# Twelve weight loads per chunk, each cut in two halves issued one step apart

## The reference

```
x = x + 0.5 * ffn(layernorm(x))
x = x + mamba(layernorm(x))
x = x + 0.5 * ffn(layernorm(x))

ffn:    xr, xk = mixes of x and of x one token earlier
        out = sigmoid(xr @ W_r.T) * ((relu(xk @ W_k.T) ** 2) @ W_v.T)
mamba:  xn = layernorm(x) * ln_w + ln_b ;  xs, z = split(xn @ W_in.T)
        xc = silu(causal conv of 4 taps over xs)
        dt_low, B, C = split(xc @ W_xproj.T) ;  delta = softplus(dt_low @ W_dt.T + b_dt)
        h[t] = exp(delta * A) * h[t-1] + delta * B * xc        (1024 channels, 16 states)
        y = sum over states(h * C) + D_skip * xc ;  out = (y * silu(z)) @ W_out.T + x
```

## Time and profile before

| what | value |
|---|---|
| runs | 4676.57, 4679.0, 4679.5 us (median 4679.0) |
| the profiled execution, its own time | 4679.25 us |
| its span, first to last instruction | 4677.5 us |
| mean granted TensorE clock | 0.974 |
| busy: PE / DVE / POOL / ACT | 4190.6 / 4202.4 / 3559.8 / 3164.0 us |
| DMA of the kernel's queue | 807.00 MB, 54.1% of the 16 engines' span |

### The profile page before, as it was taken

How to read it: one execution, slowest core, us unless ns; L and a number is a source line. 1 busy time by engine, 2 the same in 40 slices (tenths; PEclk the granted TensorE clock), 3 DMA queues, 4 the chain that set the end, 5 groups by cost and what they waited for, 6 DMA issues and landing times.

```text
span 4677.5 us, 58356 instructions
## 1 busy us (share of the span) xinstructions
PE 4190.6 (90%) x16768; PEld 2358.7 (50%) x16768; DVE 4202.4 (90%) x3266; ACT 3164.0 (68%) x6740; POOL 3559.8 (76%) x3712
## 2 busy tenths in 40 slices
PE   5777999999999999999999999999999999999787
PEld 2444555555555555555455555555555555555453
DVE  1799999999999999999999999999999999999991
ACT  3666677767767677667767767776776767766562
POOL 2677787877878778787788878787787887878771
PEclk8888999999999999999999999999999999999798
DMA  2455555555655555565555655556565555655551
GB/s 76 125 158 185 177 180 181 178 195 167 192 180 178 173 181 195 181 194 177 182 173 181 198 177 180 181 178 195 168 192 181 178 176 182 193 179 167 159 184 55
DMA packets 423058, 810.74 MB, mean 173 GB/s; under 512 B 41265, under 2 KB 41265, under 8 KB 418641
## 3 DMA queue, kind: packets, MB, share of 16 engines
q1 hardware_dynamic: 422736, 807.00, 54.1%
HBM read 772.25 MB, written 34.60 MB: 172 GB/s over the span
## 4 chain that ended last, share of the span: by engine, by line
PE 45%; DVE 24%; issue 12%; POOL 8%; ACT 7%; DMA 3%; SPq 0%; DVEq 0%; POOLq 0%; ACTq 0%
DVE decay L1099 13%; PE mm L478 9%; PE y_acc L573 9%; PE mm L489 8%; DVE g L1107 7%; POOL dbx L1306 6%; PE mm L515 5%; PE mm L500 4%; PE mm L602 3%; DVE xc L1051 3%; DMA c_all<-bc_scratch 3%; PE mm L525 3%; PE mm L537 2%; POOL xin L1295 1%; PE mm L464 1%
## 5 line engine op out<-in xcount | busy, mean ns | idle before, releaser
L1306 POOL TENSOR_TENSOR dbx<-u,b_all 128x1024 f32<-128x1024 f32 x1024 | 2417.9, 2361 | 187.0 <-DVE g L1107 183.6
L1099 DVE TENSOR_TENSOR_SCAN decay<-decay,state,dbx 128x1024 f32<-128x1024 f32 x1024 | 2406.9, 2350 | 155.2 <-ACT decay L913 131.7
L1107 DVE TENSOR_TENSOR g<-decay,c_all 128x1024 f32<-128x1024 f32 x1024 | 1246.3, 1217 | 57.7 <-PE y_acc L573 45.0
L573 PE MATMUL y_acc<-ident,g 128*128 128x128 f32 x8192 | 1077.8, 279 | 238.2 <-DVE g L1107 235.8
L573 PEld LDWEIGHTS y_acc<-ident,g 128*128 128x128 f32 x8192 | 950.3, 143 | 657.9 <-DVE g L1107 384.8
L910 ACT ACTIVATE decay<-delta,neg_a 128x512 f32<-128x512 f32 x1024 | 708.5, 692 | 37.1 <-ACT state L919 0.4
L919 ACT ACTIVATE state<-decay 128x2 f32<-128x2 f32 x1024 | 167.9, 164 | 782.5 <-DVE g L1107 780.0
L913 ACT ACTIVATE decay<-delta,neg_a 128x511 f32<-128x511 f32 x1024 | 687.1, 671 | 0.0
L500 PE MATMUL mm<-wbuf_c,col 128*128 128x512 f32 x1024 | 458.2, 593 | 9.6 <-ACT delta L861 8.2
L1051 DVE SCALAR_TENSOR_TENSOR xc<-mm,conv_sb,xc 128x509 f32<-128x509 f32 (+2 forms) x384 | 285.3, 743 | 50.4 <-ACT xs_last L825 41.4
L500 PEld LDWEIGHTS mm<-wbuf_c,col 128*128 128x128 f32 x1024 | 187.4, 190 | 214.7 <-issue 212.5
(11 more groups left out here) (107 smaller groups left out, 5377.0 us busy)
## 6 DMA issues: line engine op xcount, KB each, us to landing
b_all<-bc_scratch SPq DMA_DIRECT2D x1024, 256.0 KB, 3.7
c_all<-bc_scratch SPq DMA_DIRECT2D x1024, 256.0 KB, 4.0
wbuf_d<-in_w_r SPq DMA_DIRECT2D x32, 1024.0 KB, 7.1
wbuf_c<-in_w_v SPq DMA_DIRECT2D x32, 1024.0 KB, 7.7
xin<-in_x SPq DMA_DIRECT2D x16, 1024.0 KB, 7.0
wbuf_c<-in_w_k SPq DMA_DIRECT2D x16, 1024.0 KB, 5.6
wbuf_d<-in_w_in SPq DMA_DIRECT2D x16, 1024.0 KB, 8.2
res_scratch<-rows SPq DMA_DIRECT2D x16, 1024.0 KB, 6.2
```

What stands on the lines that cost most here:

```text
L573: last = pe.matmul(y_acc[:, tb, j * P:(j + 1) * P], g[:, s % PAIRS, j, tb * P:(tb + 1) * P], ident[:, :], start=n == 0 and j == 0 and tb % ...
L1099: dve.tensor_tensor_scan(d, d, flat(dbx[:, s % DBX, :, :]), state[:, batch, s, 0:1], ALU.mult, ALU.add).then_inc(scan_done, 1)
L1107: dve.tensor_tensor(g[:, s % PAIRS, :, :], decay[:, s % PAIRS, :, :], c_all[:, s % CRING, :].unsqueeze(1).broadcast_to([P, QT, W]), ALU.mu ...
L1306: pool.tensor_tensor(dbx[:, s % DBX, :, :], u[:, q % 2, :, :], b_all[:, s % BRING, :].unsqueeze(1).broadcast_to([P, QT, W]), ALU.mult).the ...
```

## The change

The piece of 512 x 512 becomes two of 256 rows: a helper `half` takes the place of `piece`. The first half stands where the load stood, behind the same wait. The second half is issued one step later, without a wait of its own, behind that step's `c_all` and `b_all`. Both halves add 16 to the same semaphore, and each reader waits for twice the count. This is done for all twelve loads. Three of them, and one of the readers, are shown; the others follow the same pattern.

```diff
-            def piece(dram, rows0, cols0):
-                return dram[rows0:rows0 + 512, cols0:cols0 + 512].rearrange("(t p) n -> p t n", p=P)
+            def half(dram, rows0, cols0):
+                return dram[rows0:rows0 + 256, cols0:cols0 + 512].rearrange("(t p) n -> p t n", p=P)
...
                     if back and s == LOAD["wo1"]:
                         after(mark(z_pe, b, "7"))
-                        sp.dma_start(wbuf["b"][:, :, :], piece(w_out, 512, 0)).then_inc(wo_loaded[1], 16)
+                        sp.dma_start(wbuf["b"][:, 0:2, :], half(w_out, 512, 0)).then_inc(wo_loaded[1], 16)
+                    if back and s == min(LOAD["wo1"] + 1, NSTEP - 1):
+                        sp.dma_start(wbuf["b"][:, 2:4, :], half(w_out, 768, 0)).then_inc(wo_loaded[1], 16)
                     if back and s == LOAD["res"]:
...
                     if scn and s == LOAD["wz0"]:
                         after(mark(f_pe[0], f, "v3") if front else mark(f_pe[1], it - 2, "v3"))
-                        sp.dma_start(wbuf["c"][:, :, :], piece(w_in, 0, E)).then_inc(wz_loaded[0], 16)
+                        sp.dma_start(wbuf["c"][:, 0:2, :], half(w_in, 0, E)).then_inc(wz_loaded[0], 16)
+                    if scn and s == min(LOAD["wz0"] + 1, NSTEP - 1):
+                        sp.dma_start(wbuf["c"][:, 2:4, :], half(w_in, 256, E)).then_inc(wz_loaded[0], 16)
...
                             after((f_pe[1].sem, count))
-                        sp.dma_start(wbuf["d"][:, :, :], piece(w_r, 0, 0)).then_inc(wr_loaded[1], 16)
+                        sp.dma_start(wbuf["d"][:, 0:2, :], half(w_r, 0, 0)).then_inc(wr_loaded[1], 16)
+                    if back and s == min(LOAD["wr1"] + 1, NSTEP - 1):
+                        sp.dma_start(wbuf["d"][:, 2:4, :], half(w_r, 256, 0)).then_inc(wr_loaded[1], 16)
...
-                pe.wait_ge(wo_loaded[part], 16 * (k + 1))
+                pe.wait_ge(wo_loaded[part], 32 * (k + 1))
```

More of the change, by code:

```diff
@@ L380, in body @@
                         after(mark(f_pe[0], f, "k3"))
-                        sp.dma_start(wbuf["c"][:, :, :], piece(w_v, 0, 0)).then_inc(wv_loaded[0], 16)
+                        sp.dma_start(wbuf["c"][:, 0:2, :], half(w_v, 0, 0)).then_inc(wv_loaded[0], 16)
+                    if front and s == min(LOAD["wv0"] + 1, NSTEP - 1):
+                        sp.dma_start(wbuf["c"][:, 2:4, :], half(w_v, 256, 0)).then_inc(wv_loaded[0], 16)
                     if front and s == LOAD["wxs0"]:
                         after(mark(f_pe[0], f, "r3"))
-                        sp.dma_start(wbuf["d"][:, :, :], piece(w_in, 0, 0)).then_inc(wxs_loaded[0], 16)
+                        sp.dma_start(wbuf["d"][:, 0:2, :], half(w_in, 0, 0)).then_inc(wxs_loaded[0], 16)
+                    if front and s == min(LOAD["wxs0"] + 1, NSTEP - 1):
+                        sp.dma_start(wbuf["d"][:, 2:4, :], half(w_in, 256, 0)).then_inc(wxs_loaded[0], 16)
                     if scn and s == LOAD["wz0"]:
                         after(mark(f_pe[0], f, "v3") if front else mark(f_pe[1], it - 2, "v3"))
-                        sp.dma_start(wbuf["c"][:, :, :], piece(w_in, 0, E)).then_inc(wz_loaded[0], 16)
+                        sp.dma_start(wbuf["c"][:, 0:2, :], half(w_in, 0, E)).then_inc(wz_loaded[0], 16)
+                    if scn and s == min(LOAD["wz0"] + 1, NSTEP - 1):
+                        sp.dma_start(wbuf["c"][:, 2:4, :], half(w_in, 256, E)).then_inc(wz_loaded[0], 16)
                     if back and s == LOAD["wk1"]:
                         after(mark(y_pe, b, "o3"))
-                        sp.dma_start(wbuf["b"][:, :, :], piece(w_k, 0, 0)).then_inc(wk_loaded[1], 16)
+                        sp.dma_start(wbuf["b"][:, 0:2, :], half(w_k, 0, 0)).then_inc(wk_loaded[1], 16)
+                    if back and s == min(LOAD["wk1"] + 1, NSTEP - 1):
+                        sp.dma_start(wbuf["b"][:, 2:4, :], half(w_k, 256, 0)).then_inc(wk_loaded[1], 16)
                     if front and s == LOAD["wxs1"]:
@@ L395, in body @@
                             after(mark(m_pe, f - 1, "xs7"))
-                        sp.dma_start(wbuf["a"][:, :, :], piece(w_in, 0, 512)).then_inc(wxs_loaded[1], 16)
+                        sp.dma_start(wbuf["a"][:, 0:2, :], half(w_in, 0, 512)).then_inc(wxs_loaded[1], 16)
+                    if front and s == min(LOAD["wxs1"] + 1, NSTEP - 1):
+                        sp.dma_start(wbuf["a"][:, 2:4, :], half(w_in, 256, 512)).then_inc(wxs_loaded[1], 16)
                     if front and s == LOAD["res_out"]:
@@ L402, in body @@
                         after(mark(z_pe, it, "3") if scn else mark(f_pe[1], b - 1, "v3"))
-                        sp.dma_start(wbuf["c"][:, :, :], piece(w_v, 0, 0)).then_inc(wv_loaded[1], 16)
+                        sp.dma_start(wbuf["c"][:, 0:2, :], half(w_v, 0, 0)).then_inc(wv_loaded[1], 16)
+                    if back and s == min(LOAD["wv1"] + 1, NSTEP - 1):
+                        sp.dma_start(wbuf["c"][:, 2:4, :], half(w_v, 256, 0)).then_inc(wv_loaded[1], 16)
                     if back and s == LOAD["wr1"]:
@@ L414, in body @@
                             after(mark(y_pe, b, "o3"))
-                        sp.dma_start(wbuf["a"][:, :, :], piece(w_out, 0, 0)).then_inc(wo_loaded[0], 16)
+                        sp.dma_start(wbuf["a"][:, 0:2, :], half(w_out, 0, 0)).then_inc(wo_loaded[0], 16)
+                    if scn and s == min(LOAD["wo0"] + 1, NSTEP - 1):
+                        sp.dma_start(wbuf["a"][:, 2:4, :], half(w_out, 256, 0)).then_inc(wo_loaded[0], 16)
                     if scn and s == LOAD["wz1"]:
@@ L418, in body @@
                             after(mark(f_pe[1], b, "k3"))
-                        sp.dma_start(wbuf["b"][:, :, :], piece(w_in, 0, E + 512)).then_inc(wz_loaded[1], 16)
+                        sp.dma_start(wbuf["b"][:, 0:2, :], half(w_in, 0, E + 512)).then_inc(wz_loaded[1], 16)
+                    if scn and s == min(LOAD["wz1"] + 1, NSTEP - 1):
+                        sp.dma_start(wbuf["b"][:, 2:4, :], half(w_in, 256, E + 512)).then_inc(wz_loaded[1], 16)
                     if front and s == LOAD["bc_out"]:
@@ L434, in body @@
                             after(mark(m_pe, f, "xs3"))
-                        sp.dma_start(wbuf["d"][:, :, :], piece(w_r, 0, 0)).then_inc(wr_loaded[0], 16)
+                        sp.dma_start(wbuf["d"][:, 0:2, :], half(w_r, 0, 0)).then_inc(wr_loaded[0], 16)
+                    if ahead and s == min(LOAD["wr0"] + 1, NSTEP - 1):
+                        sp.dma_start(wbuf["d"][:, 2:4, :], half(w_r, 256, 0)).then_inc(wr_loaded[0], 16)
                     if ahead and s == LOAD["wk0"]:
@@ L442, in body @@
                             after(mark(f_pe[0], f, "v3"))
-                        sp.dma_start(wbuf["c"][:, :, :], piece(w_k, 0, 0)).then_inc(wk_loaded[0], 16)
+                        sp.dma_start(wbuf["c"][:, 0:2, :], half(w_k, 0, 0)).then_inc(wk_loaded[0], 16)
+                    if ahead and s == min(LOAD["wk0"] + 1, NSTEP - 1):
+                        sp.dma_start(wbuf["c"][:, 2:4, :], half(w_k, 256, 0)).then_inc(wk_loaded[0], 16)
                     if back and s == LOAD["out"]:
@@ L472, in ffn_k @@
                 pe.wait_ge(f_pool[i].sem, f_pool[i].at(k, "xk3"))
-                pe.wait_ge(wk_loaded[i], 16 * (k + 1))
+                pe.wait_ge(wk_loaded[i], 32 * (k + 1))
                 if free := bank_free(it, f"f{i}k{j}"):
@@ L483, in ffn_r @@
                 pe.wait_ge(f_pool[i].sem, f_pool[i].at(k, "xr3"))
-                pe.wait_ge(wr_loaded[i], 16 * (k + 1))
+                pe.wait_ge(wr_loaded[i], 32 * (k + 1))
                 if free := bank_free(it, f"f{i}r{tb}"):
@@ L494, in ffn_v @@
                 pe.wait_ge(f_act[i].sem, f_act[i].at(k, "sq3"))
-                pe.wait_ge(wv_loaded[i], 16 * (k + 1))
+                pe.wait_ge(wv_loaded[i], 32 * (k + 1))
                 if free := bank_free(it, f"f{i}v{tb}"):
@@ L509, in xs @@
                 pe.wait_ge(m_act.sem, m_act.at(k, "xn3"))
-                pe.wait_ge(wxs_loaded[e // 4], 16 * (k + 1))
+                pe.wait_ge(wxs_loaded[e // 4], 32 * (k + 1))
                 if free := bank_free(it, f"xs{e}"):
@@ L519, in z @@
             def z(it, k, e, slot):
-                pe.wait_ge(wz_loaded[e // 4], 16 * (k + 1))
+                pe.wait_ge(wz_loaded[e // 4], 32 * (k + 1))
                 if free := bank_free(it, f"z{e}"):
```

## The result

The changed kernel takes 4723.25 us (median of 4 runs, 4713.08 to 4724.68) against 4677.78 us before (4674.07 to 4679.5). The ratio is 1.0094, 95% interval 1.0076 to 1.0111: 45 us slower, where the forecast was 21 and the range ended at 4721. Four further runs of the same kernel had a median of 4718.19 us (4713.24 to 4722.01) against 4679.68, ratio 1.0082 (1.0068 to 1.0096): 38.5 us. In two sets of the experiments a single execution stood far off (6438.78 us with `wo1` alone split, 9112.23 us with the half moved between `c_all` and `b_all`), and the ratios go by the others alone. The profiled execution is the quickest of the first four, 4713.1 us with a span of 4711.3 us, 33.8 us above the span of before.

The account below looks back on a forecast made before the run. PE and DVE, each 90% busy, were taken to bound the kernel, with nobody waiting for `c_all`. 4679.25 us plus 21 for fourteen waits at `wo1`, all other terms nothing, gave 4700 us; range 4680 to 4721.

Parts of the forecast that it names:

- The place and the path: PE waits for `wo1`'s second half before a pass's first `wbuf_b` matmul; the delay reaches DVE's multiply in full: 21 us.
- the other places: Second halves of the other eleven weights: cost nothing, with up to 1 us allowed at `wr1` in the last scanned chunk.
- SP's issues: Twelve more DMA issues a pass on SP, 6 us of 278 on a queue that mostly waits: cost nothing.
- the late `xout`: Load of `xout` leaves 0.5 us later; up to 1 us a pass of new DVE idle time, costing nothing.
- the 3% of the chain for `c_all`: Some 140 us put down to `c_all` transfers, read as no wait; rival that it is real: 4654 us, chance 0.06.
- the wait is then 5.5 - 4.1 = 1.4 us, and 0.1 for PE to start again: At `wo1`: landing 5.5 us after `b_all`, first use 4.1 us after it; 1.5 us a pass with the restart.
- The follower `xout`: 1 MB load right behind `wo1`'s second half; may slow its landing to 6.9 us, counted only at the upper end.
- the 5.5 of the estimate: Landing of `wo1`'s second half, in us from the `b_all` before it: 7.2 for a 1 MB load, less 1.7.
- 14 x 1.5 us: Fourteen full passes, each with 1.5 us of PE wait at `wo1`, with no slack found: 21 us.
- The last scanned pass: The one pass where `wr1` has less time before its first use: up to 1 us allowed, inside the range.
- The drain: Final part, where the scan does not hold SP back: the halves leave together, cost put at nothing.
- The large case: Rival: `xout` slows `wo1`'s second half to 6.9 us; 2.8 + 0.1 us a pass, 41 us, 4720 us; chance 0.12.

Follow-up runs that it names:

- the kernel with a wait of 3.7 us a pass: Kernel before with the whole load of `wo1` issued in step 4 in place of step 3, nothing split: 4763.15 us, ratio 1.0182.

## Why the prediction was wrong in size

**The place and the path were right.** Fourteen waits before the first matmul with `wbuf_b`, released by the landing, reaching DVE at the multiply that had waited 0.60 us; the other places free; SP's issues and the late `xout` free; the 3% of the chain for `c_all` no wait. The kernel with `wo1` whole gives all of it back but 3 us, which its interval does not tell from nothing; the one with `wo1` alone split has 36.5 of it by the medians.

**The wait was mis-sized.** The step "the wait is then 5.5 - 4.1 = 1.4 us, and 0.1 for PE to start again" measured 5.9 - 4.2: 24.6/14 = 1.76 us in the first profile, 23.5/14 = 1.68 in the second, and the 0.1 for starting again is there (3.70 against 3.60 us for the eight matmuls). The follower `xout`, which I had left to the upper end, is the difference: without it the half landed at 5.35, near the 5.5 of the estimate (the lines of `xout` one step later show it in one execution; the landings of the two kernels overlap, 4.5 to 6.3 and 4.7 to 5.6 us). This adds 14 x 0.36 = 5 us.

**The step that failed outright is a missing term: what PE does after it has waited.** I costed 14 x 1.5 us as if PE resumed at the speed it had. In passes in which the granted clock fell behind the wait, the eight matmuls took 5.40 to 6.75 us. In the two profiles of the changed kernel the matmuls with `wbuf_b` are busy for 4.4 and 8.2 us more, 1.4 of it the restarts and 3.0 and 6.8 the clock, and the kernel with a wait of 3.7 us a pass shows the term in every pass, 28.6 us with its restarts. In the profiles of the changed kernel the term is no larger than the mis-sized wait (3.0 and 6.8 us against 5); it differs in that the prediction has no place for it. The row that should have warned me was in the trace of before: some 15 us ahead of this place the clock stands at the lower level for 3.3 us, in a stretch in which that costs little because PE has small transposes to do (kernel before, the same columns as in the earlier trace rows; then PE's timeline just ahead of it):

```profile
2107.60:2110.90 3.30, 3.30 (x18) 3.30 (x17) 3.15 (x3) 3.11 (x9) 1.74 (x2) 0.50 0.45 137
```

```profile
2105.63 1.06 PE L464 MATMUL mm<-ident,rows 128*128 128x128 f32 x8 [1.41 <-DVE gate L1056]
```

PE had been idle for 1.41 us there too. That was ground enough to give a new wait, in front of tens of us of dense work on the path, a term of its own.

**The last scanned pass.** I allowed up to 1 us, though my own reckoning gave more: there the first use of `wr1` stands 3.8 us behind the `b_all` in the kernel before, and 5.5 - 3.8 = 1.7. In the changed kernel PE waits 2.00 us before it and in the kernel before not at all; the half is issued at 4509.80 and lands 4.9 us later, 0.1 us ahead of the matmul at 4514.80.

**The drain.** I put it at nothing. From the last scan to the end the changed kernel takes 112.3 us and the kernel before 109.9. No load is waited for there; a stretch of 6.8 us at the lower clock lies over the first output projection, where the kernel before has the upper one (1.00). PE's timelines, before and then changed, and the changed kernel's clock:

```profile
4576.04 3.67 PE L602 MATMUL mm<-wbuf_a,gate 128*128 128x512 f32 x8 [0.99 <-DVE gate L1062]
...
4608.19 5.68 PE L626 MATMUL mm<-wbuf_a,gate 128*128 128x512 f32 x8 [0.83 <-DVE gate L1086]
```

```profile
4605.80:4612.60 6.80, 5.97 (x14) 3.19 (x13) 1.38 (x2) 0.00 (x0) 0.00 (x0) 0.53 0.11 46
```

These 2.4 us are not a price of the waits at `wo1`: two variants in which PE waits for no `wbuf_b` have them too (`wo1` one step earlier and the half between `c_all` and `b_all`, 112.3 us each), and the kernel with `wo1` alone split has not (109.8).

**The sum.** 24.6 + 4.4 + 2.0 + 2.4 = 33.4 of the 33.8 us of the profiled execution. In the second profile it is 23.5 + 8.2 + 1.7 + 2.6 = 36.0 of 37.6 us, and that execution (4717.03 us) stands 1.2 us below the median of its set. Against the 21 us of the forecast the first profile has 12.8 us more: 5 from the size of the wait, 3.0 from the clock behind it, 2.0 from `wr1`, 2.4 from the drain. The matmuls of `dt_proj` are busy for 147.6 us in the changed kernel and for 141.3 before as well, without one more; by this sum little of it reaches the end. The 10 us between that execution and the median of its set, 4723.25, are not assigned; they decide whether the measured time lies inside the range, and no trace shows them.

**The rivals.** The large case came near the measured time (4720) by luck in good part: the follower is real, but costs 0.6 us and not 1.4, and its waits of 2.8 us a pass were 1.7; the clock, `wr1`, the drain and the 10 us that are not assigned make up the rest. By the fit in the Trainium skill (DMA: Bandwidth & Descriptors, the anatomy of one DMA, for transfers issued from GpSimd: 2.0 us and the bytes at 436 GB/s) the half would, as an estimate, have come in 3.2 us. The trace disagrees: issued from SP, it took 4.5 at the least and 5.6 in the median.

## What to carry to other kernels

When a transfer is cut in two and a piece moves later in a queue, the price is at the consumer with the least time between the new place and its first use: list that distance for every consumer, in time and not in steps, since the queue may stand in a wait between the two. A chain that names a DMA is a question, not an answer: look whether the reader was idle. And a new wait on TensorE in front of dense matmuls is to be costed with the matmuls behind it at the lower clock in some or all passes: here 1.6 to 3.2 us for eight of them, in 1 to 4 of fourteen passes behind waits of some 2 us and in all fourteen behind waits of some 4.

## What the runs showed of the hardware

- Two loads of 512 KB back to back, for one of 1 MB, made no difference in time (ratio 1.0002, 0.9993 to 1.0010).
- A wait of TensorE of 0.3 to 2.8 us was followed by matmuls at the lower clock in 1, 2 and 4 of fourteen passes (three profiles) and in 1 of the twelve with a wait (`xout` a step later); one of 2.95 to 4.65 us in all fourteen; without a wait it happened in none of 84 passes (six profiles). Within the first group the length of the wait did not sort the passes: 2.22 us had it, 2.52 did not. Of the eight passes with slow matmuls in that group, six had a clock of 0.99 or 1.00 over the 20 us ahead. What else decides was not settled.
- A 1 MB transfer issued 0.9 us behind a 512 KB one delayed the smaller one's landing by 0.6 us in the mean (5.9 against 5.35 us from the `b_all` ahead of both), though it stands behind it in the same queue. One execution without it stands behind this.
